# Transposing attention probabilities on VectorE instead of TensorE, with casts, low halves and two products in other places

## What is computed

```python
h = film(rmsnorm(x, norm1_w), cond, film1_w, film1_b)
Q = h @ q_w + q_b
K = h @ k_w + k_b
V = h @ v_w + v_b
scores = jnp.einsum('bnd,bmd->bnm', Q, K) * D ** (-0.5)
attn = jax.nn.softmax(scores, axis=-1)
out = jnp.einsum('bnm,bmd->bnd', attn, V)
x = x_in + (out @ proj_w + proj_b)
x_in = x
h = film(rmsnorm(x, norm2_w), cond, film2_w, film2_b)
h = jax.nn.gelu(h @ mlp_w1 + mlp_b1, approximate=False) @ mlp_w2 + mlp_b2
return x_in + h
```

## Time and profile before

| | |
|---|---|
| Median of three runs | 1762.76 us |
| Profiled execution, its own time | 1765.63 us |
| Span of its instructions | 1763.8 us |
| TensorE busy | 1750.1 us, 99% |
| Weight loads of TensorE | 1468.9 us, 83% |
| VectorE busy | 1254.7 us, 71% |
| ScalarE busy | 888.1 us, 50% |
| GpSimd busy | 205.7 us, 12% |
| Mean granted TensorE clock | 0.997 of full speed |

### The profile page before, as it was taken

How to read it: one execution, slowest core, us unless ns; L and a number is a source line. 1 busy time by engine, 2 the same in 40 slices (tenths; PEclk the granted TensorE clock), 3 DMA queues, 4 the chain that set the end, 5 groups by cost and what they waited for, 6 DMA issues and landing times.

```text
span 1763.8 us, 23169 instructions
## 1 busy us (share of the span) xinstructions
PE 1750.1 (99%) x8308; PEld 1468.9 (83%) x8308; DVE 1254.7 (71%) x1749; ACT 888.1 (50%) x1490; POOL 205.7 (12%) x202
## 2 busy tenths in 40 slices
PE   8899999999999999999999999999999999999998
PEld 7788888888888888888888888888888888888887
DVE  5867677565665787588578758858875885885476
ACT  5454545545454555455455445545544554653344
POOL 0578685000000000000000000000000000000000
PEclk9999999999999999999999999999999999999999
DMA  9586868633226678768777866876786677677675
GB/s 335 163 297 249 291 256 274 245 99 112 78 102 199 201 250 277 207 203 276 249 197 250 280 202 207 274 248 197 262 267 201 220 269 243 191 244 240 193 233 194
DMA packets 202307, 395.83 MB, mean 224 GB/s; under 512 B 24145, under 2 KB 28241, under 8 KB 200145
## 3 DMA queue, kind: packets, MB, share of 16 engines
q1 hardware_dynamic: 202192, 394.34, 68.8%
HBM read 331.25 MB, written 62.98 MB: 224 GB/s over the span
## 4 chain that ended last, share of the span: by engine, by line
PE 96%; DMA 2%; DVE 1%; ACT 1%; SPq 0%; POOL 0%; issue 0%; DVEq 0%
PE psum L687 35%; PE psum L707 23%; PE psum L587 14%; PE psum L715 12%; PE psum L657 3%; PE psum L615 3%; PE psum L616 3%; PE psum L620 3%; DMA norm_row<-rs_scratch 1%; DMA rs_scratch<-rstd 1%; DMA x_tok<-x_dram 1%; DVE h L1053 0%; ACT x_tok L803 0%; PE psum L601 0%; PE psum L648 0%; DVE h L1046 0%
## 5 line engine op out<-in xcount | busy, mean ns | idle before, releaser
L687 PE MATMUL psum<-op_hi_P,ring 128*128 128x512 f32 x1792 | 552.0, 389 | 0.0
L707 PE MATMUL psum<-stage_hi,ring 128*128 128x512 f32 x1792 | 442.5, 389 | 0.0
L707 PEld LDWEIGHTS psum<-stage_hi,ring 128*128 128x128 f32 x1792 | 336.3, 188 | 69.8
L687 PEld LDWEIGHTS psum<-op_hi_P,ring 128*128 128x128 f32 x1792 | 336.1, 188 | 69.6
L888 ACT CAST stage_hi<-x 128x1024 fp32r<-128x1024 f32 x224 | 235.4, 1054 | 235.2 <-PE psum L707 223.0
L687 PE MATMUL psum<-op_lo_P,ring 128*128 128x512 f32 x896 | 348.6, 389 | 0.0
L1266 DVE TENSOR_TENSOR stage_lo<-x,stage_hi 128x1024 fp32r<-128x1024 f32 x224 | 273.6, 1225 | 72.3 <-ACT stage_hi L888 72.1
L872 ACT ACTIVATE x<-x,vecs 128x512 f32<-128x512 f32 x192 | 138.1, 723 | 283.9 <-DVE x L1253 283.9
L715 PE MATMUL psum<-stage_lo,ring 128*128 128x512 f32 x896 | 239.5, 389 | 0.0
L687 PEld LDWEIGHTS psum<-op_lo_P,ring 128*128 128x128 f32 x896 | 168.2, 188 | 35.0
L715 PEld LDWEIGHTS psum<-stage_lo,ring 128*128 128x128 f32 x896 | 168.2, 188 | 34.9
(11 more groups left out here) (154 smaller groups left out, 2240.4 us busy)
## 6 DMA issues: line engine op xcount, KB each, us to landing
ring<-wu_scratch SPq DMA_DIRECT2D x448, 256.0 KB, 3.1
ring<-wd_scratch SPq DMA_DIRECT2D x448, 256.0 KB, 2.9
x_tok<-x_dram SPq DMA_DIRECT2D x16, 1024.0 KB, 10.9
xT_in<-xT_dram SPq DMA_DIRECT2D x16, 1024.0 KB, 8.2
x2T_scratch<-xT_in SPq DMA_DIRECT2D x32, 512.0 KB, 3.4
hn<-x2T_scratch SPq DMA_DIRECT2D x32, 512.0 KB, 5.6
xres<-x2T_scratch SPq DMA_DIRECT2D x32, 512.0 KB, 5.0
out_dram<-xres SPq DMA_DIRECT2D x32, 512.0 KB, 4.4
```

The source lines that it names most:

```text
L687: mm = pe.matmul(to, wt, b, start=q in FRESH and t == 0, stop=t == len(steps) - 1, skip_group_check=True)
L707: mm = pe.matmul(bank(q, dt), a[:, dt, part, :], stage_hi[r][:, e, :], start=q in FRESH and ss == 0 and e == 0 and part == 0, stop=False, ...
```

## The change

The probabilities are transposed by VectorE. `transpose_probs` moves from TensorE's stream to VectorE's, directly behind the scaling of the probabilities, as 16 instructions a group. Each takes 32 partitions with 32 columns of all four blocks (128 elements a partition), transposes the 32 by 32 squares and writes them to another 32 partitions of `pT_sb`. Their end is a semaphore of its own, `pT_done`; the copy by ScalarE and the semaphores `pT_full` and `pT_read` are gone. The PSUM bank (`key_ps`) holds only the key row now, and the key row waits for the diagonals of the group before (`key_col_done`) in place of the copy.

Three things stand in other places. ScalarE casts h of the next group ahead of the exponents, and the squares come behind these. VectorE forms the low halves of h ahead of the maxima. TensorE does g product 1 of the next group directly behind g product 0, ahead of all outputs, except in the last group, where the product P6 stays between outputs 1 and 2.

```diff
-            def transpose_probs(n):
-                pe.wait_ge(probs_scaled, n + 1)
-                wait_used(pe, pT_read, n)
-                for b in range(GB):
-                    mm = pe.transpose(pT[:, tokens(b)], probs[:, b, :], ident[:])
-                mm.then_inc(pT_full, 1)
-
             def output(n, d):
                 if d == 0:
-                    pe.wait_ge(pT_read, n + 1)
+                    pe.wait_ge(pT_done, n + 1)
                     pe.wait_ge(v_read, GB * n + GB)
                 wait_used(pe, out_read, GB * n + d - 1)
...
-                transpose_probs(n)
                 if n < LAST:
                     g_product(n + 1, 0)
+                    g_product(n + 1, 1)
...
                 output(n, 1)
-                if n < LAST:
-                    g_product(n + 1, 1)
-                else:
+                if n == LAST:
                     up(0, 0, "P6")
                 output(n, 2)
...
-                if 0 < n <= LAST - 3:
-                    sum_squares(n + 3)
+                if n < LAST:
+                    for k in range(KD):
+                        h_high(n + 1, k)
                 act.wait_ge(bias_done, n + 1)
                 for b in range(GB):
                     nc.scalar.activation(probs[:, b, :], score_b[:, b, :], ACT.Exp, bias=exp_bias[:, b:b + 1],
                                          scale=SCALE, accum_out=den[:, b:b + 1]).then_inc(exp_done, 1)
-                if n < LAST:
-                    for k in range(KD):
-                        h_high(n + 1, k)
-                if n == 0:
-                    sum_squares(3)
+                if n <= LAST - 3:
+                    sum_squares(n + 3)
...
-                act.wait_ge(pT_full, n + 1)
-                nc.scalar.copy(pT_sb[:], pT).then_inc(pT_read, 1)
...
+            def transpose_probs(n):
+
+                dve.wait_ge(probs_scaled, n + 1)
+                wait_used(dve, out_full, GB * n)
+                for i in range(0, P, 32):
+                    for j in range(0, P, 32):
+                        last = dve.transpose(pT_sb[j:j + 32, :, i:i + 32], probs[i:i + 32, :, j:j + 32])
+                last.then_inc(pT_done, 1)
...
                 key_column(n)
+                if n < LAST:
+                    wait_used(dve, v_full, GB * n)
+                    for k in range(KD):
+                        h_low(n + 1, k)
                 dve.wait_ge(scored, n + 1)
...
+                transpose_probs(n)
                 if n < LAST:
-                    wait_used(dve, v_full, GB * n)
-                    for k in range(KD):
-                        h_low(n + 1, k)
                     key_terms(n + 1)
```

More of the change, by code:

```diff
@@ L161, in cond_block_kernel @@
         g, v = at(72, "g", [P, KD, TOK]), at(80, "v", [P, GB, D])
-        probs, pT_sb = at(88, "probs", [P, GB, P]), at(90, "pT_sb", [P, TOK])
+        probs, pT_sb = at(88, "probs", [P, GB, P]), at(90, "pT_sb", [P, GB, P])
         key_bias, key_lo = at(92, "key_bias", [P, TOK]), at(92, "key_lo", [P, TOK], F32R)
@@ L191, in cond_block_kernel @@
         gv = [ps[2 * j] for j in range(KD)]
-        score, pT, out_ps = ps[1], ps[3], (ps[5], ps[7])
+        score, key_ps, out_ps = ps[1], ps[3], (ps[5], ps[7])
         film_ps = [ps[1].rearrange("p (j b) -> p j b", j=2 * KD), ps[7].rearrange("p (j b) -> p j b", j=2 * KD)]
@@ L262, in cond_block_kernel @@
             sem(n) for n in ("g_full", "g_read", "v_full", "v_read", "scored", "top_done", "bias_done", "exp_done"))
-        rden_done, probs_scaled, pT_full, pT_read, out_full, out_read = (
-            sem(n) for n in ("rden_done", "probs_scaled", "pT_full", "pT_read", "out_full", "out_read"))
+        rden_done, probs_scaled, pT_done, out_full, out_read = (
+            sem(n) for n in ("rden_done", "probs_scaled", "pT_done", "out_full", "out_read"))
         w_src_loaded, w_mixed, w_hi, w_split = (sem(n) for n in ("w_src_loaded", "w_mixed", "w_hi", "w_split"))
@@ L632, in key_row @@
                 pe.wait_ge(key_lo_done, n + 1)
-                wait_used(pe, pT_read, n)
-                product(pT, [(ones_r[:], key_hi[:]), (ones_r[:], key_lo[:])], key_row_full)
+                wait_used(pe, key_col_done, GB * n)
+                product(key_ps, [(ones_r[:], key_hi[:]), (ones_r[:], key_lo[:])], key_row_full)
             def scores(n):
@@ L656, in output @@
                 for b in range(GB):
-                    mm = pe.matmul(out_ps[d % 2][:, tokens(b)], v[:, b, tokens(d)], pT_sb[:, tokens(b)],
+                    mm = pe.matmul(out_ps[d % 2][:, tokens(b)], v[:, b, tokens(d)], pT_sb[:, b, :],
                                    start=True, stop=True)
@@ L1080, in key_column @@
                 dve.wait_ge(key_row_full, n + 1)
-                wait_used(dve, pT_full, n)
+                wait_used(dve, pT_done, n)
                 for b in range(GB):
-                    dve.tensor_tensor_reduce(probs[:, b, :], pT[:, tokens(b)], ident[:], 1.0, 0.0, ALU.mult, ALU.add,
+                    dve.tensor_tensor_reduce(probs[:, b, :], key_ps[:, tokens(b)], ident[:], 1.0, 0.0, ALU.mult, ALU.add,
                                              key_col[:, b:b + 1]).then_inc(key_col_done, 1)
```

## The result

The changed kernel takes 1814.1, 1814.2 and 1822.0 us (a fourth execution was disturbed and counts for nothing); the ratio to the kernel before (median 1762.82) is 1.0303, with a 95% interval of 1.0288 to 1.0318. It is slower, as forecast, but by four times as much: 13 us were forecast, the range ended at 1795. The profiled execution is the one of 1822.0, with a span of 1820.2, against 1763.8: 56.4 us more.

A forecast was written before the change was run, and what follows sets the result against it. TensorE, 96% of the chain, was taken to bound the kernel. Terms 8.5 - 1.5 + 2.5 + 1.2 - 0.3 + 2.6 gave +13.0, hence 1778.6 profiled and 1775.8 us as median, range 1756 to 1795.

The forecast's parts named there:

- TensorE's own work: TensorE from transposes to outputs' end: 9.43 us a group becomes 8.84, saving 0.59, of which 0.35 are the transposes.
- the wait between outputs: Output 2 waits for VectorE's add of output 0, sharing its bank: 0.3 us in each of the first 15 groups.
- Transposes: Sixteen VectorE transposes a group at 0.24 us each: 3.8 us, between 2.7 and 23.
- rival 5: VectorE's transposes wait for GpSimd, one instruction each: 0.95 us apiece, 15.2 a group, total 1867 us; chance 0.07.
- When VectorE reaches the first add: VectorE, groups 1 to 7: first add at S + 16.0, 1.5 us late, costing +1.2 a group, +8.5 in all.
- S: Zero point for times within a group: the moment VectorE starts the maxima, 304.97 in group 8 before the change.
- The stall: TensorE's wait at output 2 for the first add in groups 1 to 7: 1.8 us each, less 0.59 saved.
- T: Start of output 0 on TensorE, forecast at S + 13.43; output 2 wanted at T + 1.71.
- Group 0: Low halves ahead of the maxima push the probabilities by about 3 us: +2.6, between -1 and +5.
- Late maxima in groups 1 to 7: VectorE's low halves, beside GpSimd's sums, end about S + 3.6, delaying the maxima by 3.6 us.
- Groups 13 and 14: First add about 1.4 us late in group 13 and 2.8 in group 14: +1.2 and +2.5.
- Rival 4: VectorE's transposes dearer, 0.35 us each, 1.8 more in ten groups: 1793 us; chance 0.13.

The follow-up runs named there:

- e8: Kernel before the change, with only both g products of the next group put ahead of the outputs: 1767.4 us, ratio 1.002.
- e6: Changed kernel with VectorE's first two adds of groups 0 to 7 put ahead of the next group's key terms: 1782.8 us, ratio 1.011.
- e2: Changed kernel with casts, squares and low halves of h back in their old places, low halves directly ahead of the transposes: 1815.6 us, ratio 1.0293.
- e1: Changed kernel with g product 1 put back between outputs 1 and 2: 1802.9 us, ratio 1.022.
- e7: Kernel before the change, with only the casts and low halves moved ahead of the maxima: 1770.5 us, ratio 1.0035.
- e3: Changed kernel with transposes back on TensorE and the copy on ScalarE, the other moves kept: 1773.6 us, ratio 1.0054.
- e5: Changed kernel with 16 unread matmuls added between outputs 1 and 2 of groups 1 to 7: 1803.9 us, ratio 1.0228.
- e9: Changed kernel with output 2 moved to the key row's bank, so only output 3 waits for the first add: 1802.2 us, ratio 1.0217.
- e11: Changed kernel, first two adds ahead of key terms except groups 10 and 15, group 0's low halves behind the exponentials' bias: 1779.3 us, ratio 1.0087.

## Why the prediction was right and wrong

- **TensorE's own work and the wait between outputs**: right. Net -0.29 forecast for a free group, -0.245 measured; the 0.3 for output 2 was found in e8.
- **Transposes**: the step "The nearest row in elements are the quiet modulations, 8 in 2.13, 0.27 apart. I take 0.24" failed. Sixteen take 5.05, 0.316 each, not 3.8. The modulation's rows overlap; the transposes' do not (303 ns long and 0.316 apart). The Trainium skill, "VectorE: DVE Perf Modes", section "The three transpose paths", gives 311 ns for a 128x128 one in bf16 that works only within the 32 by 32 blocks. The 303 ns here, for float32 and 32 partitions by 128 elements, are within 3% of it. What the Trainium skill advises on the same page, section "Rules for kernel authors", to use TensorE for a full 128x128 one, was right here too.
- **No contention of transposes with GpSimd** (rival 5): rightly given little. 299 to 310 ns everywhere.
- **When VectorE reaches the first add**: the mechanism was right, the time was not. Forecast S + 16.0; in group 6, with S = 277.80 from TensorE's scores, it came at 296.75 = S + 18.95. The 2.95 between are: 1.3 the transposes; 0.45 the maxima (4.05 late, not 3.6); 0.6 because 13.5 was a middle of groups and group 6 had 14.1; 0.7 the key terms, 4.82 from first start to the adds here and 4.14 before (255.14 to 259.28), which the forecast had not costed again. That they now meet other GpSimd work may be why; no run shows it. The small additions took about the 0.5 they were given. Group 6 is one of the later ones: over groups 1 to 7 the first add came at S + 18.0 to S + 19.1.
- **The stall**: 1.8 forecast, 3.54 measured. S + 18.95 would have made it 4.8, but output 0 came late too, at S + 14.15 and not S + 13.43 (0.34 of it because the g product ahead of it waited for v and ran late). It starts 0.05 behind the last transpose's end. "The probabilities themselves are in time, transposed near S + 12.5" failed by 1.6, and with it T. TensorE's wait is then no longer counted from the scores: from the start of output 0 to the end of the first add it is the key terms and the add, 5.60, less the 2.05 of outputs 0 and 1, 3.55. That is why it is 3.54 or 3.55 in six groups of eight, in all of which output 0 starts within 0.1 of the last transpose's end, and why putting the adds first (e6) removes it.
- **The clock**: missing altogether, a term that the sum put at nothing without a reason. It held nothing for what follows a wait, and in the profiled execution that is 20 of 56.4 us, 15.9 in groups 0 to 7 and 4.2 in groups 13 and 14. In the kernel before TensorE's longest wait from the first transposes of group 0 on was 1.80, with full clock behind it. The Trainium skill tells of it, in "TensorE: Matmul & The Clock Gate", section "HAM oscillation — how this bites in real kernels": a loop that lets TensorE idle once per tile (there for a DMA) brings its clock down in every tile. The changed kernel's trace agrees, with 0.50 behind each of its eight waits of 3.25 to 3.55 us; e2's does in part, since two waits of 3.56 and 3.57 left the clock up. With the forecast's stall, 1.8, there would probably have been nothing of it: no wait of 0.8 to 1.80 in the groups of these runs was followed by half clock, though one of 1.92 (e1) was. So the size of the stall seems to have decided twice.
- **Group 0**: +2.6 forecast, counted to the third g product. That starts at 85.66 where it was 83.29, +2.4: right. Half clock behind the wait of 3.25 then costs 1.0 more on this product. The low halves alone cost 3.1 there, half clock included (e7).
- **Late maxima in groups 1 to 7** were right: 3.6 forecast, 3.1 to 4.2 measured. Alone they cost 0.33 a group and not the 1 of e7's expectation.
- **Groups 13 and 14**: +1.2 and +2.5 forecast as 1.8 and 3.1 of stall; the waits were 2.59 and 4.30, and both were followed by half clock. Group 12 waited 0.86 for the first add and group 15 1.69 for its transposes, which the forecast put at nothing and at 1 at most. The 1.3 that a group's transposes take beyond the forecast is about what these waits are too long by.
- Rival 4, dearer transposes at 0.35, was the nearest and gave 1793. Its transposes were too dear and its total too low, since it had no clock and no late key terms.

## What to carry to other kernels

When an engine off the path is given work, walk its whole order from the event that starts it to every event that somebody waits for, with that engine's own longest rows, and then ask which of those events each waiter's time is counted from; as soon as one is late, the next stall is set by what stands between the two, here key terms between transposes and adds. Price a stall of the bounding TensorE in two parts, the wait and the stretch at half clock behind it, and check in the windows which of the two a given length brings. Work that releases somebody goes ahead of work that nobody waits for yet: that order alone was worth 40 us of span here (e6), where taking the transposes off VectorE was worth 49 (e3).

## What the runs showed of the hardware

- A wait of the same length had different results for the clock. 2.59 in group 13 of the changed kernel was followed by half clock (the four outputs' second pair took 3.68), 2.60 in the same group of e5 was not (2.05). In e1 2.44 was not, but 2.42 and 1.92 were; in e9 2.01, 2.18 and all four of 2.65 were, and 1.91 was not. The eight waits of 3.25 to 3.55 in the changed kernel all were, but in e2 one of 3.56 and one of 3.57 were not, and 3.33 in e11 was not. Which rule decides is open; length alone does not. The wait of 3.56, with sixteen output matmuls at full clock behind it (2.05):

```profile
152.50 2.05 PE L650 MATMUL psum<-pT_sb,v 128*128 128x128 f32 x16 [3.56 <-DVE xT_in L1089]
```

- In group 6 the half clock began while TensorE still waited (0.50 from 296) and lasted some 5 us behind the wait, though TensorE was busy from its end. In groups 5 and 7 it began with the wait's end or just behind it and was over before the next g product (2.84 for that product).
- A float32 VectorE transpose of 32 partitions by 128 elements takes 303 ns, one of 128 partitions by 512 takes 711 ns. So sixteen that move squares across partitions cost 5.05 us, and a single one that doesn't, over the same elements, a seventh of that.
- Filling a wait with useless matmuls made the kernel 0.7% faster than waiting idle (ratio 1.0228 in place of 1.0303).
